# A selective-scan kernel: a second quad of states by token on ScalarE in every second group, and one ring of eight slots

## What is computed

```python
def _mamba_dir(h, W_in, conv_w, conv_b, Wx, Wdt, bdt, A_log, Dp, W_out):
    xz = jnp.einsum('bld,ed->ble', h, W_in)
    x, z = (xz[..., :Di], xz[..., Di:])            # Di = 256 channels
    x = _silu(causal_conv(x, conv_w) + conv_b)     # 4 taps
    x_dbl = jnp.einsum('bld,ed->ble', x, Wx)       # step (64), B (16), C (16)
    dt = jax.nn.softplus(jnp.einsum('blr,dr->bld', dt, Wdt) + bdt)
    A = -jnp.exp(A_log)                            # 256 channels x 16 states
    dA = jnp.exp(dt[..., None] * A)
    dBx = (dt * x)[..., None] * Bm[:, :, None, :]
    def step(hc, inp):
        hc = dA_t * hc + dBx_t
        return (hc, jnp.einsum('bdn,bn->bd', hc, C_t))
    y = (scan over tokens) + x * Dp
    y = y * _silu(z)
    return jnp.einsum('bld,ed->ble', y, W_out)
x = layernorm(x + fwd(x) + flip(rev(flip(x))))
x = layernorm(x + ffn(x))          # ffn: norm, clip at the largest value, ternary weight
```

## Time and profile before

| | us |
|---|---|
| median of 3 runs (lowest, highest) | 878.61 (874.13, 881.37) |
| span of the profiled execution, first to last instruction | 875.2 |
| first scan of group 0 starts | 35.30 |
| last scan ends | 836.2 |

### The profile page before, as it was taken

The page is one execution under the profiler, slowest core; times in us unless marked ns, Lnnn a source line. Parts: engine busy times, 40 slices in busy tenths (PEclk is TensorE's granted clock), DMA queues, the critical chain, the costliest instruction groups (busy, mean ns, idle before and its releaser), DMA issues. The chain is left out here.

```text
span 875.2 us, 9930 instructions
## 1 busy us (share of the span) xinstructions
PE 644.4 (74%) x2650; PEld 262.4 (30%) x2650; DVE 796.6 (91%) x816; ACT 654.4 (75%) x1147; POOL 794.2 (91%) x391
## 2 busy tenths in 40 slices
PE   8577786967778795867787795878788696568474
PEld 5232231413333231313333231323333131223223
DVE  3379999999999999999999999999999999999866
ACT  3588787877879787876888787876888786865514
POOL 0398999999998999999998999999998999998925
PEclk9989796979989798979889798989989897966778
DMA  3885746474765745583775656484675557385003
GB/s 68 173 191 108 160 97 144 87 160 79 174 137 121 168 88 119 97 185 76 153 163 109 152 93 135 84 190 93 130 162 107 121 104 154 75 180 181 25 0 97
DMA packets 82103, 108.12 MB, mean 124 GB/s; under 512 B 43648, under 2 KB 56960, under 8 KB 81792
## 3 DMA queue, kind: packets, MB, share of 16 engines
q1 hardware_dynamic: 82048, 107.49, 57.6%
HBM read 33.80 MB, written 6.55 MB: 46 GB/s over the span
## 5 line engine op out<-in xcount | busy, mean ns | idle before, releaser
L582 POOL TENSOR_TENSOR dbx<-step_rep,bc_rep 128x1024 f32<-128x1024 f32 x192 | 452.5, 2379 | 14.6 <-DMA step_rep<-step 12.1
L835 ACT ACTIVATE da_ps<-step_rep,neg_a 128x512 f32<-128x512 f32 x384 | 257.7, 690 | 95.5 <-DVE hs L1109 94.5
L592 POOL TENSOR_TENSOR ch<-hs,bc_rep 128x1024 f32<-128x1024 f32 x120 | 284.9, 2375 | 19.9 <-DVE hs L1109 15.3
L1109 DVE TENSOR_TENSOR_SCAN hs<-da_ps,dbx 128x512 f32<-128x512 f32 x192 | 220.5, 1204 | 24.4 <-ACT da_ps L835 12.0
L1109 DVE TENSOR_TENSOR_SCAN hs<-da_ps,carry,dbx 128x512 f32<-128x512 f32 x192 | 232.6, 1264 | 5.9 <-ACT da_ps L835 5.9
L1369 PE MATMUL y_ps<-ch,stack 128*32 128x512 f32 x1024 | 158.1, 693 | 91.4 <-POOL ch L592 53.2
L761 ACT ACTIVATE dbx_tok<-c_ps,b_cols 128x256 f32<-128x256 f32 x256 | 111.0, 489 | 27.2 <-PE c_ps L1421 22.4
L1360 PE MATMUL c_ps<-x_dbl,select 128*128 128x512 f32 x160 | 105.2, 745 | 33.7 <-DVE ch L1020 27.0
L1020 DVE TENSOR_TENSOR ch<-hs,c_ps 128x2048 f32<-128x2048 f32 x56 | 126.6, 2261 | 0.0
L1308 PE MATMUL pre<-h_t,w_conv 128*128 128x512 f32 x248 | 113.6, 600 | 7.5 <-ACT xs L713 5.8
L1433 PE MATMUL da_ps<-ident,dbx_tok 128*128 128x128 f32 x512 | 76.6, 284 | 33.6 <-DVE hs L1109 32.4
(11 more groups left out here) (188 smaller groups left out, 606.7 us busy)
## 6 DMA issues: line engine op xcount, KB each, us to landing
step_rep<-step SPq DMA_DIRECT2D x256, 256.0 KB, 5.4
bc_rep<-bc_rows SPq DMA_DIRECT2D x96, 256.0 KB, 5.1
...
```

The costliest lines, as they stand in the source:

```text
L582: nc.gpsimd.tensor_tensor(dbx[:, j % DBX_RING], dtx_rep[:, r], b_rep[:, s % 2, k, :].unsqueeze(1).to_broadcast([P, 2, CHUNK]), ALU.mult).t ...
L592: nc.gpsimd.tensor_tensor(ch[:, n % RING], hs[:, n % RING], c_rep[:, s % 2, k, :].unsqueeze(1).to_broadcast([P, 2, CHUNK]), ALU.mult).then ...
L835: nc.scalar.activation(bank, dt_rep[:, r, e, :], ACT.Exp, scale=neg_a[:, half_of(unit), 2 * (unit % 2) + e, g, k:k + 1]).then_inc(da_ready, 1)
L1109: nc.vector.tensor_tensor_scan(in_scan_order(hs[:, n % RING, e, :], s), in_scan_order(factor, s), in_scan_order(term, s), initial, ALU.mul ...
```

## The change

It does six things together.

1. In g1 and g3 quad 2 is also worked by token: units 4, 5, 14 and 15 in addition to 6, 7, 10 and 11. ScalarE scales 16 activations per part there instead of 8, TensorE turns eight units instead of four, GpSimd makes 8 products dtx*B instead of 12.
2. `POOL_C` lists 8, 9, 8, 9 units instead of 7, 8, 7, 8, and other ones: 34 of the 64 units of a batch instead of 30. VectorE's 30 others form 14 pairs and 2 lone units (before: 14 pairs and 6 lone ones).
3. One ring of eight slots holds a unit's dtx*B or, by token, its exponentials; the scan writes the states over them in place. A slot is free when the C product of the unit eight back is done and, in g0 and g2, its last column kept (`wait_slot`). VectorE no longer waits for the C product four back. `dbx`, `hs` and `da_sb` are gone.
4. The B columns are turned on chip: at step 6 TensorE transposes the B rows of `x_dbl` into `c_ps[:, 1]` (`turn_b`, which waits until the tokens of the group ahead are scaled), at step 8 ScalarE copies 32 columns (`copy_b`). The four DMAs per group are gone.
5. `EXPS_AFTER` moves some exponentials ahead of other work of ScalarE.
6. The first layer norm's result is written in place over `resid`, and `h_res` is loaded in halves, which gives back SBUF. VectorE's residual now waits until the last result is stored.

```diff
-RING = 4
+RING, CH_RING = 8, 4
-EXPS_AFTER = ((2, 4, 6, 8, 10, 14, 14, 16, 18, 24, 24, 24, 26, 28, 30, 32),
-              (2, 4, 6, 8, 10, 14, 14, 16, 18, 24, 24, 24, 26, 28, 30, 32),
+EXPS_AFTER = ((2, 4, 6, 8, 10, 16, 16, 16, 18, 24, 24, 24, 26, 28, 30, 32),
+              (2, 4, 6, 10, 12, 16, 16, 16, 18, 24, 24, 24, 26, 28, 30, 32),
...
-TOKEN_QUADS = ((3,),) * NG
+TOKEN_QUADS = ((3,), (2, 3), (3,), (2, 3))
+B_TURNED, B_COPIED = 6, 8
-POOL_C = ((0, 1, 3, 8, 9, 12, 13),
-          (0, 2, 4, 5, 8, 9, 12, 13),
-          (0, 1, 4, 5, 9, 12, 13),
-          (0, 1, 4, 5, 8, 9, 12, 14))
+POOL_C = ((0, 1, 4, 5, 8, 9, 12, 13),
+          (0, 1, 4, 5, 8, 9, 12, 13, 14),
+          (0, 1, 4, 5, 8, 9, 12, 13),
+          (0, 1, 4, 5, 8, 9, 12, 13, 14))
+        def wait_slot(eng, i):
+            if i >= RING:
+                b, s, n = unit_of(i - RING)
+                wait_c_product(eng, b, s, n)
+                if s in (0, 2):
+                    eng.wait_ge(carried, UNITS * (2 * b + s // 2) + n + 1)
...
-                        load_b_cols(*nxt)
-                j = pool_b(b, s, n)
-                if j >= DBX_RING:
-                    pool.wait_ge(scanned, scan_of_pool_unit(j - DBX_RING) + 2)
-                nc.gpsimd.tensor_tensor(dbx[:, j % DBX_RING], dtx_rep[:, r],
+                i = unit(b, s, n)
+                wait_slot(pool, i)
+                nc.gpsimd.tensor_tensor(ring[:, i % RING], dtx_rep[:, r],
...
+            def copy_b(b, s):
+                act.wait_ge(b_turned, NG * b + s + 1)
+                nc.scalar.copy(b_cols[:, s % 2], c_ps[:, 1, 0:TT * STATES].rearrange("p (t n) -> p t n", t=TT)[:, :, QUAD * FIRST_TOKEN_QUAD:]
...
                 if e:
                     dve.wait_ge(xn_ready, TT * e)
-                    dve.wait_ge(x1_ready, TT * e)
+                    dve.wait_ge(x1_stored, 16 * e)
...
                             if e == 0:
                                 if not by_token(s, n):
                                     dve.wait_ge(dbx_ready, pool_b(b, s, n + 1))
-                                if n >= RING:
-                                    wait_c_product(dve, b, s, n - RING)
-                                elif group:
-                                    wait_c_product(dve, *before(b, s), n - RING + UNITS)
...
+            def turn_b(b, s):
+                pe.wait_ge(x_dbl_sb, group + 1)
+                (and for the tokens of the group ahead to be scaled)
+                for t in range(TT):
+                    ins = nc.tensor.transpose(c_ps[:, 1, t * STATES:(t + 1) * STATES], x_dbl[0:STATES, s % 2, t * P:(t + 1) * P],
+                                              ident[0:STATES, 0:STATES])
```

More of the change, by code:

```diff
@@ L589, in times_c @@
                 pool.wait_ge(scanned, 2 * (UNITS * group + n + 1))
-                if not (group == 0 and n < RING):
-                    pool.wait_ge(summed, UNITS * group + n - RING + 1)
-                nc.gpsimd.tensor_tensor(ch[:, n % RING], hs[:, n % RING],
+                if not (group == 0 and n < CH_RING):
+                    pool.wait_ge(summed, UNITS * group + n - CH_RING + 1)
+                nc.gpsimd.tensor_tensor(ch[:, n % CH_RING], ring[:, unit(b, s, n) % RING],
                                         c_rep[:, s % 2, k, :].unsqueeze(1).to_broadcast([P, 2, CHUNK]),
@@ L822, in batch @@
                             if by_token(s, unit):
[L823 to L826 removed]
+                                i = UNITS * group + unit
+                                bank = ring[:, i % RING, e, :]
+                                if e == 0:
+                                    wait_slot(act, i)
                             elif half >= DA_BANKS:
@@ L869, in batch @@
                             nc.scalar.preload_act_table_set(EXP)
+                        if n == B_COPIED and not (last and s == NG - 1):
+                            copy_b(*following(b, s))
                         for f in range(2):
@@ L1006, in times_c @@
                 dve.wait_ge(scanned, 2 * (UNITS * group + n + 1))
-                if not (group == 0 and n < RING):
-                    dve.wait_ge(summed, UNITS * group + n - RING + 1)
-                nc.vector.tensor_tensor(ch[:, n % RING], hs[:, n % RING],
+                if not (group == 0 and n < CH_RING):
+                    dve.wait_ge(summed, UNITS * group + n - CH_RING + 1)
+                nc.vector.tensor_tensor(ch[:, n % CH_RING], ring[:, unit(b, s, n) % RING],
                                         c_ps[:, 0, :].unsqueeze(1).to_broadcast([P, 2, CHUNK]),
@@ L1406, in output_product @@
                 ins.then_inc(o_ps, 1)
+            def turn_b(b, s):
+                group = NG * b + s
+                pe.wait_ge(x_dbl_sb, group + 1)
+                if group:
+                    of = before(b, s)
+                    for k in TOKEN_QUADS[of[1]]:
+                        pe.wait_ge(tokens_scaled[k], products(*of, k))
+                else:
+                    pe.wait_ge(u_taken, 2)
+                for t in range(TT):
+                    ins = nc.tensor.transpose(c_ps[:, 1, t * STATES:(t + 1) * STATES], x_dbl[0:STATES, s % 2, t * P:(t + 1) * P],
+                                              ident[0:STATES, 0:STATES])
+                ins.then_inc(b_turned, 1)
             def take_tokens(b, s, f):
@@ L1500, in batch @@
                             take_tokens(b, s, 1)
+                        if n == B_TURNED and not (last and s == NG - 1):
+                            turn_b(*following(b, s))
                         if n == TOKENS_TAKEN[0] and not (last and s == NG - 1):
```

116 lines of the change are left out of this document (47 added, 69 removed), and 4 rows, old and new, of the table EXPS_AFTER.

## The result

The changed kernel takes 906.45 us in the median of four runs (904.18 to 908.1); the kernel before took 879.28 beside it. The ratio is 1.031, 95% interval 1.027 to 1.036: 3.1% slower, where I had forecast 862 and faster, and above my range. Ratios stand against the kernel before, timed beside each run on the same chip, with a 95% interval.

The account below looks back on a forecast made before the run. It took VectorE and GpSimd, both full and coupled through ScalarE and TensorE, as the bound. 875.2 - 14 (four batches) - 2 (start) = 859.2, median 3.4 above: 862 us; the mechanism's own range 855 to 869, the whole range up to 884.

Parts of the forecast that it names:

- Busy times: Per batch, VectorE falls from 191.96 to 187.5 us and GpSimd from 195.3 to 185.8; ScalarE gains 32 scalings.
- my bound of 3.2: Lower bound in us for a lot of eight added ScalarE scalings, taken as 3.4, upper bound 3.9.
- g0's second half and g1's first: This stretch becomes ScalarE's own: 50.8 us plus 0.7 of waiting, 51.5 against 50.4, or +1.1 per batch.
- rival 2: ScalarE keeps idling 4.1 us for TensorE in g1's first half; stretch +4.6, total 877 us; chance 0.19.
- The other six halves: Rest of a batch period: ScalarE stays below VectorE, which loses 4.5 us; 149.06 becomes 144.4 us.
- Rival 3: In odd groups TensorE turns unit 5 too late; on top of rival 2, +15, 892 us; chance 0.13.
- The start: Before the first scans, waits for the B column DMAs and second quad of B go: gain 2 us, bounds 0 and 2.5.
- At nothing: The ring, the halves of `h_res`, the norm in place and the tail were costed at nothing.
- Rival 1: GpSimd was the pacer; VectorE then bounds at 191.2 us per batch, -8.2, total 844 us; chance 0.16.

Follow-up runs that it names:

- e5: Changed kernel with 7 of 8 scalings of quad 2 left out in the last three of four batches: 900.59 us, ratio 1.021.
- e1: Changed kernel with the next group's x_dbl product at TensorE's step 14 instead of 13: 893.89 us, ratio 1.015.
- e9: Changed kernel with x_dbl at step 14 and GpSimd's dtx*B four units ahead of the scan instead of three: 886.83 us, ratio 1.006.
- e14: e9 with the old table of C products in g0 and g2, new exponentials kept: 878.01 us, ratio 0.998.
- e16: e14 with units 2 and 3 instead of 4 and 5 on GpSimd for C products in g1 and g3: 909.91 us, ratio 1.035.
- e2: Changed kernel with one token quad in every group and the old tables of C products and exponentials: 880.64 us, ratio 1.003.

## Why the prediction was wrong

**Busy times: right for two engines.** VectorE 188.29 us per batch (187.5), GpSimd 186.57 (185.8). ScalarE got 11.1 more per batch, not 15: all scalings took 160.0 us in the run instead of 111.0, 0.38 for each of the 128 that were added, and eight of these make 3.1, just below my bound of 3.2. Part of that runs beside ScalarE's neighbouring instructions.

**g0's second half and g1's first: right sum, wrong reason.** Forecast +1.1 us, measured 49.94 against 48.31, +1.6. This is luck: it is +2.4 in g0 and -0.8 in g1. (My 50.4 began at unit 7; from unit 8 on ScalarE has 21.19 of 23.56 us, and the same sum gives +1.2.) I held that ScalarE bounds there; e5 took 4.4 us from it and nothing changed. From unit 6 to unit 10 a chain of TensorE and ScalarE sets the length, and the pair product had left it. ScalarE's idling for the turned dtx went, 2.21 to 0.42 us, so rival 2 did not come.

**The step that failed:** "The other six halves keep ScalarE below VectorE ... VectorE loses 4.5 in them, and I leave its waits nearly as they are: 144.4". With units counted from unit 8, they took 151.3 before and 158.2 after. I had compared busy times of engines per half and never walked TensorE's queue at the end of an odd group, where two more units had to be turned, nor GpSimd's where its products fell away. The runs put in place of that term: TensorE's queue at units 14 and 15, 1.6% (e1), GpSimd's hole, 0.9 (e9 against e1), the table of C products, 0.6 (e14 against e9). In this order they add up to the 3.1% lost against the kernel before. They are not clean shares: ScalarE's scalings, which I had counted as covered in the other halves, are worth 1.0% by e5, also in g3, where GpSimd's hole costs; how these two overlap no run shows. And they do not explain the whole miss. The time is 44 us above the forecast, and 27 of them are loss; the other 17, the gain that I had forecast, came in no run.

**Rival 3 had the right kind of mechanism at the wrong unit.** Unit 5 waited 0.35 us in g1 in the changed kernel (second batch). There the pair product covers; e16 took it away, and the wait became 4.71 us. The cover shrank by 2.3, and the projection and the start of the sum took 2.07 + 2.97 us instead of 1.04 + 1.88, 2.1 more, at a granted clock of 0.50 instead of 1.00: together the 4.4 us. Unit 15 has no such product in front: from the end of unit 13's first half VectorE has 1.2 + 2.4 = 3.6 us of scans, TensorE 1.1 + 3.3 + 1.1 us and half of its own turn, 0.5. I had that arithmetic and used it at unit 5 only, not at unit 15, where it would have shown the loss.

**The start: right.** The first scan began at 35.7 us (35.3 before), but the first period was only 2.5 us longer than the second, before 4.7: 1.8 us net. That is one profile of each, and the first scan began anywhere from 35.3 to 39.0 us in the runs.

**At nothing: nearly right.** The ring, the turn of B and the norm in place cost 0.3%, 0.6 at most (e2).

**Rival 1** did not come: in the changed kernel GpSimd is busy 759 us instead of 794 and in e14 740, and neither is faster than before. Whether GpSimd paced the kernel before, and another wait took its place, no run isolates. **Still open** is why e14, with VectorE at 190.3 us of a 199.7 us period, is no faster than before. It has 50 us of idle time ahead of scans against 44; what is new against before are the waits of unit 15 of g1 and g3 (5.6 us together), of units 10 and 6 of g0 (4.8 and 4.5) and of unit 5 of g3 (4.2). No run isolates them.
